# Cross-attention on one core: the first shift in halves, outputs two batches behind, products with V in one block a batch

## The reference

```python
Q = (query @ Wq.T + bq).reshape(B, Sq, N_HEADS, D_K).transpose(0, 2, 1, 3)
K = (key_value @ Wk.T + bk).reshape(B, Skv, N_HEADS, D_K).transpose(0, 2, 1, 3)
V = (key_value @ Wv.T + bv).reshape(B, Skv, N_HEADS, D_K).transpose(0, 2, 1, 3)
scores = jnp.einsum('bhqd,bhkd->bhqk', Q.astype(jnp.float32), K.astype(jnp.float32))
scores = scores / np.sqrt(D_K)
attn = jax.nn.softmax(scores, axis=-1)
context = jnp.einsum('bhqk,bhkd->bhqd', attn, V.astype(jnp.float32)).astype(query.dtype)
...
output = context @ W_o.T + b_o
x = output + query
mu = jnp.mean(x, axis=-1, keepdims=True)
var = jnp.mean(jnp.square(x - mu), axis=-1, keepdims=True)
return (x - mu) / jnp.sqrt(var + LN_EPS) * ln_gamma + ln_beta
```

## Time and profile before

| | us |
|---|---|
| median of 3 runs | 155.61 (154.75 to 156.13) |
| profiled execution, whole | 157.02 |
| its span on the core | 155.2 |

### The profile page before, as it was taken

One profiled execution on the slowest core, in us unless ns is written; L12 is line 12 of the kernel. 1 busy time (PEld: TensorE's weight loads), 2 busy tenths in 40 slices (PEclk: granted clock), 3 DMA queues, 4 the chain that ended last, 5 costly groups with the idle time before them and its releaser, 6 DMA issues.

```text
span 155.2 us, 3853 instructions
## 1 busy us (share of the span) xinstructions
PE 134.0 (86%) x1466; PEld 116.7 (75%) x1466; DVE 105.6 (68%) x247; ACT 80.4 (52%) x163; POOL 60.7 (39%) x83
## 2 busy tenths in 40 slices
PE   5799989679979999889998998999899996779850
PEld 4599779468768899769988987899787875667620
DVE  6745997757937769947896699578779887031252
ACT  3648437214426666526655666465656565566410
POOL 8946997920003998404140504130023023041051
PEclk9999999987999999999999999999999999999997
DMA  4976989698950250697414050405031001001002
GB/s 128 358 259 216 269 296 227 159 270 239 301 204 2 102 156 0 169 267 235 135 52 151 4 178 4 155 2 183 24 128 34 4 4 30 4 4 30 4 0 59
DMA packets 14354, 19.58 MB, mean 126 GB/s; under 512 B 2192, under 2 KB 13520, under 8 KB 14336
## 3 DMA queue, kind: packets, MB, share of 16 engines
q1 hardware_dynamic: 13056, 17.26, 35.6%
q0 software_dynamic: 592, 1.70, 4.5%
q10 hardware_dynamic: 688, 0.38, 0.8%
HBM read 6.30 MB, written 0.92 MB: 47 GB/s over the span
## 4 chain that ended last, share of the span: by engine, by line
PE 65%; DVE 11%; DMA 10%; ACT 6%; issue 5%; SPq 1%; POOLq 0%; ACTq 0%; DVEq 0%
PE m_bank L793 19%; PE pv_bank L873 12%; PE st_bank L857 11%; PE mx_bank L834 10%; DMA q_stack<-shift 6%; DVE mx L656 6%; PE m_bank L901 4%; DMA c_raw<-ctxT 3%; PE m_bank L884 2%; ACT pw L561 2%; PE st_bank L793 2%; DMA q_stack<-q_first 1%; DVE q_hl L618 1%; PE m_bank L841 1%; ACT o_normT L552 1%
## 5 line engine op out<-in xcount | busy, mean ns | idle before, releaser
L656 DVE TENSOR_REDUCE mx<-mx_bank 112x1 f32<-112x375 f32 x128 | 64.6, 541 | 20.4 <-PE mx_bank L834 19.8
L561 ACT ACTIVATE pw<-st_bank 125x448 f32<-125x448 f32 x90 | 48.5, 548 | 48.5 <-PE st_bank L857 47.7
L834 PE MATMUL mx_bank<-k_stack,q_stack 128*112 128x376 f32 x128 | 41.3, 351 | 2.2 <-DVE mx L656 1.2
L857 PE MATMUL st_bank<-q_stack,k_stack 128*125 128x224 f32 x180 | 37.7, 294 | 1.7 <-DMA q_stack<-shift 1.7
L857 PEld LDWEIGHTS st_bank<-q_stack,k_stack 128*125 128x125 f32 x180 | 30.0, 190 | 5.5 <-issue 3.0
L834 PEld LDWEIGHTS mx_bank<-k_stack,q_stack 128*112 128x112 f32 x128 | 22.0, 181 | 4.5 <-DVE mx L656 2.4
L359 POOL TENSOR_TENSOR c_hl<-c_raw,c_hl 128x752 fp32r<-128x752 f32 x6 | 10.9, 1814 | 27.5 <-DVE c_hl L612 27.5
L873 PE MATMUL pv_bank<-pw,v_sb 125*17 125x112 f32 x720 | 20.4, 260 | 1.1 <-ACT o_raw L535 1.1
L405 POOL TENSOR_SCALAR var_eps<-mv 112x1 f32<-112x1 f32 x7 | 1.6, 223 | 49.2 <-DVE mv L692 49.2
L793 PE MATMUL m_bank<-c_hl,w_hl 128*128 128x376 f32 x84 | 18.7, 365 | 0.9 <-ACT w_hl L449 0.9
L873 PEld LDWEIGHTS pv_bank<-pw,v_sb 125*17 125x17 f32 x720 | 16.3, 97 | 3.9 <-issue 2.2
(11 more groups left out here) (102 smaller groups left out, 160.6 us busy)
## 6 DMA issues: line engine op xcount, KB each, us to landing
k_stack<-k_hl SPq DMA_DIRECT2D x48, 188.0 KB, 2.5
c_raw<-ctxT SPq DMA_DIRECT2D x8, 375.0 KB, 4.3
q_stack<-q_hl SPq DMA_DIRECT2D x6, 224.0 KB, 4.5
q_stack<-q_hl SPq DMA_DIRECT2D x6, 168.0 KB, 3.4
x_space<-x_nat POOLq DMA_DIRECT2D x1, 896.0 KB, 10.3
out<-yo SPq DMA_DIRECT2D x8, 112.0 KB, 1.9
pw<-wT SPq DMA_DIRECT2D x2, 256.0 KB, 4.8
x_space<-xT SPq DMA_DIRECT2D x1, 448.0 KB, 6.1
```

The lines of the kernel that those rows point to most:

```text
L561: nc.scalar.activation(p_tile[0:KC, n % PR, :, :], st_of(n)[0:KC, 0:4 * Q].rearrange("p (j q) -> p j q", j=4), ACT.Exp, scale=float(DK) ** ...
L656: nc.vector.tensor_reduce(mx[b % 2][:, h % 2, q_pair(h // 2):q_pair(h // 2) + 1], mx_bank[n % MR][0:Q, 0:KV], axis=AX_X, op=ALU.max, negat ...
L834: nc.tensor.matmul(mx_bank[n % MR][0:Q, 0:KVP], q_stack[k][:, side, q_pair(h // 2), b - Q_STACKS[k][0], :], k_stack[b % 3][:, h // 2, :], ...
L857: last = nc.tensor.matmul(st_of(n)[0:KC, k * 2 * Q:(k + 1) * 2 * Q], k_stack[i % 3][:, 2 * g + k, c * KC:(c + 1) * KC], q_stack[qk][:, :, ...
```

## The change

**Order tables.** P's ring gets fourteen tiles. yo is dropped (z is scaled in place), which frees the space.

```diff
-PR = 3 * NC
+PR = UNITS + 2
...
-U_K = (0, 2)
-U_V = (3, 5, 8)
-U_OT, U_ONT, U_OUT = 5, 9, 11
-U_BIAS = 4
-U_Q = (5, 10)
-U_NEGATE, U_MT, U_SHIFT = 5, 7, 9
-U_CONTEXT = 7
-HEADS = (1, 1, 2, 1, 2, 1, 1, 1, 2, 1, 2, 1)
...
+U_OUT, U_OT, U_BIAS = 2, 8, 1
+U_K = (3, 5)
+U_V = ((11, 11, 11), (10, 11, 11), (9, 10, 11))
...
+NORM_WITH = {3: 0, 4: 1, 5: 2, 6: 4, 7: 5}
+U_MT = (11, 9, 6, 6, 6, 6, 6)
+U_NEGATE = (10, 8, 5, 5, 5, 5, 5)
...
+EARLY_HEADS = 14
...
+FIRST_JOBS = {1: (("MT", 0, 1), ("V", 2, 0)), 2: (("V", 2, 1),), 3: (("V", 2, 2),), 4: (("Q", 2, 0),), 5: (("Q", 2, 1),)}
+FIRST_K = (6, 8)
...
-FIRST_HEADS = (2, 3, 2, 3, 2)
+HEADS = (2, 1, 1, 1, 2, 1, 1, 1, 2, 1, 2, 1)
+FIRST_HEADS = ((2, 1, 2, 2, 2, 2, 2, 2, 2, 1, 1, 1), (2, 2, 2, 2, 2, 2, 2, 1, 2, 2, 2, 2))
```

```diff
+            def negate_half(t):
+
+                dve.wait_ge(max_read, H // 2 * (t + 1))
+                src = mx[0][:, :, t:NP:2]
+                hi = neg_half[t][:, :, 0, :]
+                nc.vector.tensor_tensor(hi, src, src, op=ALU.max).then_inc(neg_hi, 1)
+                dve.wait_ge(neg_hi, t + 1)
+                nc.vector.tensor_tensor(neg_half[t][:, :, 1, :], src, hi.bitcast(F32), op=ALU.subtract).then_inc(neg_ready, 1)
...
+            def take_shift_half(t):
+                src = wait_full(dve, "MT", 0, t)
+                nc.vector.tensor_copy(shift_half[t][:, :], src[0:2 * NP, 0:Q]).then_inc(shift_ready, 1)
...
+            def stack_shift_half(t):
+
+                act.wait_ge(shift_ready, t + 1)
+                for side in range(2):
+                    act.dma_start(q_stack[0][SPREAD - 1:2 * SPREAD:SPREAD, side, t:NP:2, 0, :].bitcast(F32),
+                                  shift_half[t][NP * side:NP * (side + 1), :].bitcast(F32)).then_inc(half_in[t], 16)
...
-            stack_shift(0)
-            v_part(2, 1)
+            stack_shift_half(0)
+            v_part(1, 1)
+            context_hi(3)
+            for t in range(2):
+                k_hi_part(2, t)
...
-            negate(0)
-            take_shift(0)
...
+                if n == H // 2 - 1:
+                    negate_half(0)
+                if n == H // 2 + 1:
+                    take_shift_half(0)
+                if n == 12:
+                    k_lo_part(2, 0)
...
+            def transpose_max_half(t):
+                dst, full = claim("MT", 0, t)
+                pe.wait_ge(neg_ready, t + 1)
+                nc.tensor.transpose(dst[0:2 * NP, 0:Q], neg_half[t][:, :, :, :].rearrange("q s l a -> q (s l a)").bitcast(F32),
+                                    ident[0:Q, 0:Q]).then_inc(full, 1)
...
-                if u == 0:
-                    pe.wait_ge(shift_in[i % 2], 16 * (i // 2 + 1))
+                if i == 0 and u % HALF == 0:
+                    pe.wait_ge(half_in[u // HALF], 32)
+                if i >= 1 and u == 0:
+                    pe.wait_ge(shift_in[i % 2], 16 * ((i + 1) // 2))
```

```diff
+            def subtract_k(b, t):
+
+                pool.wait_ge(k_hi, 2 * b + t + 1)
+                nc.gpsimd.tensor_tensor(k_hl[b % 2][:, 1, t, :], k_full[:, t, :], k_hl[b % 2][:, 0, t, :].bitcast(F32),
+                                        op=ALU.subtract).then_inc(k_lo, 1)
...
+            def take_k(b, t):
+
+                src = wait_full(act, "K", b, t)
+                if b > AHEAD:
+                    act.wait_ge(k_lo, 2 * (b - 1) + t + 1)
+                nc.scalar.activation(k_full[:, t, :], src[:, 0:KVP], ACT.Identity,
+                                     bias=bqk[:, 2 + t:3 + t]).then_inc(k_taken, 1)
+                act.wait_ge(k_taken, 2 * (b - AHEAD) + t + 1)
+                act.wait_ge(k_in[(b - 2) % 3][t], 48 * ((b - 2) // 3 + 1))
+                nc.scalar.copy(k_hl[b % 2][:, 0, t, :], k_full[:, t, :]).then_inc(k_hi, 1)
```

```diff
+                if b in NORM_WITH:
+                    norm_columns(dst, NORM_WITH[b])
...
-                    elif u % (2 * NC) == 1 + late and n > 2 and not (i == B - 1 and u > 2):
-                        for group in (n // NC - 2, n // NC - 1):
-                            values(*divmod(group, NG))
...
+                    elif u == (1 if i < B - 1 else 2) and i >= 1:
+                        for group in range(NG):
+                            values(i - 1, group)
+                    if i == 0:
+                        for kind, *at in FIRST_JOBS.get(u, ()):
+                            projects[kind](*at)
+                    if u == U_BIAS and i == 1:
+                        bias_of_values()
+                    if u == U_OUT and 3 <= i <= 5:
+                        out_project(i - 3)
+                    if u == U_OT and 1 <= i <= 4:
                         transpose_o(i - 1)
...
+                    if u == 4 and i in (5, 6):
+                        transpose_o(i - 1)
+                    if u == 4 and i == 5:
+                        transpose_o_norm(3)
+                    if i + 1 < B and u == U_MT[i]:
                         transpose_max(i + 1)
...
+                    if u == 7 and i == 5:
+                        out_project(3)
+                    if u == 10 and i >= 5:
+                        out_project(i - 1)
+                    if u == 5 and i == B - 1:
+                        transpose_o(B - 2)
+                    if u == 8 and i == B - 1:
+                        transpose_o_norm(B - 2)
```

```diff
+                    if u == 1 and i == 0:
+                        stack_shift_half(1)
...
+                    if u == (2 if i < B - 1 else 3) and i >= 1:
+                        take_o(i - 1)
+                    if u == (6 if i == 0 else 2) and i + AHEAD + 1 < B:
+                        context_hi(i + AHEAD + 1)
+                    if u in (FIRST_K if i == 0 else U_K) and i + AHEAD < B:
+                        take_k(i + AHEAD, (FIRST_K if i == 0 else U_K).index(u))
+                    if i + 1 < B and u == min(U_MT[i] + 1, UNITS - 1):
                         stack_shift(i + 1)
...
+                        if i + 1 in NORM_WITH:
+                            take_o_norm_t(NORM_WITH[i + 1], "MT", i + 1)
+                    if u == 5 and i == 5:
+                        take_o_norm_t(3, "ONT", 3)
+                    if u == 8 and i == B - 1:
+                        take_o_norm_t(B - 2, "ONT", B - 2)
...
+                pool.wait_ge(rstd_ready, b + 1)
+                nc.gpsimd.tensor_scalar(z[b % 2][:, :], z[b % 2][:, :], mv[b % 2][:, 0:1], rstd[:, 0:1],
+                                        op0=ALU.subtract, op1=ALU.mult).then_inc(y_ready, 1)
...
+                    if u == U_OUT and 3 <= i <= 5:
+                        layer_norm(i - 3)
+                    if i + 1 < B and u == U_NEGATE[i]:
+                        negate(i + 1)
+                    if i + 1 < B and u == U_MT[i]:
+                        take_shift(i + 1)
+                    if u == U_OT and 1 <= i <= 4:
...
-                        negate(i + 1)
+                    if u == 4 and i in (5, 6):
+                        normalise(i - 1)
+                    if u == 5 and i == B - 1:
+                        normalise(B - 2)
+                    if u == 7 and i == 5:
+                        layer_norm(3)
+                    if u == 10 and i in (5, 6):
+                        layer_norm(i - 1)
```

271 lines of the change are left out of this document (124 added, 147 removed).

## The result

The change makes the kernel slower. Four executions took 165.2 to 167.5 us, median 166.15; four of the kernel before, taken on the same chip beside them, have the median 155.69. The ratio is 1.069, with a 95% interval from 1.059 to 1.078. Forecast were 156.0 and a range that ended at 158.6. The profiled execution took 165.2, with a span of 163.3 us against 155.2. Some executions of every kernel run at a lower granted clock and take longer: the ratios and intervals leave them out, the medians do not.

What follows compares the result with a forecast made beforehand. TensorE's work and few waits bound batches 2 to 4, VectorE nearly batch 5, chains batches 6 and 7. Batch 6 at 124.2 + 23.2 + tail 8.2 = 155.6 against 155.2; median 155.61 + 0.4 = 156.0, range 152.8 to 158.6.

Steps and rivals of the forecast that it cites:

- The price list and the walk through the queue: Whole kernel: unit costs read from the trace, walked through TensorE's queue batch by batch; span 155.6 us.
- the start: Before the loop: the first half-shift, issued at 24.7, lets batch 0 begin at 28.9 us instead of 32.92.
- The o_normT waits: In front of output projections: waits for ScalarE's copy, 0.7 us each, 3.5 in five places, disappear in batches 2 to 4.
- The second step of K: ScalarE, units 2 to 5: an added cast of each K half out of SBUF, taken as 0.5 us.
- exp is late at unit 8: Batches 2 to 4: TensorE's shifted-score pair waits for ScalarE's exp, 0.7 to 0.8 us, 1.0 in batch 2.
- The layer norms do pile up: Batch 5: three layer norms instead of one, 1.0 us each on VectorE, make it 14.4 us against 11.23.
- GpSimd's new work ... is hidden.: Ten subtractions (0.9 us each) and seven row scalings on GpSimd cost nothing, since their results are read much later.
- I leave the lower clock in: + 1.7.: Batch 0: the half-rate stretch of the kernel before stays, adding 1.7 us, to 19.8 in all.
- waits of 1.8 and 1.75 in batch 0: TensorE waits 1.8 us for the first half-shift before batch 0, 1.75 at the second half's transposition.
- Landing 3.6.: Start: the first half-shift takes 3.6 us from issue to use, plus 0.6 for the second issue.
- The slower rival: ScalarE becomes the bound, with 8.2 us more work bunched behind the product block; median 159.0, chance 0.28.
- Faster, same and slower: Outcomes against the kernel before: faster case 153.5 (0.30), own sum 156.0 (0.42), slower 159.0 (0.28), regrouped by 1% bounds.

Runs made afterwards that it cites:

- bare run: The profiled execution of e_quiet_fill: the changed kernel with nearly all GpSimd hold-ups, transfers in the way of shifts and clock falls taken away; median 156.16 us.
- e_bias_late: Changed kernel with GpSimd's eight bias additions put behind the subtractions of K in batch 1; median 164.98 us, ratio 1.057.
- e_probe_ts: Kernel before plus idle GpSimd operations on one tile and two numbers beside VectorE's split of the maxima; one execution, 154.68 us.
- e_split: Changed kernel with the products with V of batches 1 to 6 in two blocks, at units 1 and 3; median 173.74 us, ratio 1.114.
- e_quiet: Changed kernel with late bias additions, GpSimd's subtraction waiting for the first half's split, and x loaded in batch 2; median 161.05 us, ratio 1.031.
- e_quiet_fill: e_quiet plus idle matmuls on TensorE in front of four waits (10, 4, 6, 3); median 156.16 us, ratio 1.002.
- e_fill: Changed kernel plus idle matmuls in front of five long TensorE waits (15, 4, 7, 8, 4); median 163.89 us, ratio 1.041.
- e_one_transfer: Changed kernel with each half-shift sent as one transfer instead of two; median 165.09 us, ratio 1.052.
- e_k_back: Changed kernel with K's low part for batches 3 to 7 back on VectorE, ScalarE in one step, no GpSimd subtraction; median 167.48 us, ratio 1.069.

## Why the prediction was wrong, step by step

**What held.** The price list and the walk through the queue. In the bare run batch 0 took 17.98 (the sum without lost clock was 18.1), batch 1 17.32 (17.3), batches 2 to 4 43.26 (43.8), batch 5 14.41 (14.4), batches 6 and 7 23.71 (23.2), the tail 8.20 (8.2). Only the start did not come out, 30.52 against 28.9. That the bare span of 155.4 agrees with the forecast 155.6 is luck in part: the forecast holds 1.7 of lost clock that the bare run does not have, and 1.6 less for the start. The o_normT waits went. The second step of K costs 0.51 (taken as 0.5) and exp is late at unit 8 by 0.47 (taken as 0.7 to 0.8). That ScalarE would become the bound did not happen. The layer norms do pile up in batch 5.

```profile
L397 POOL TENSOR_TENSOR k_hl<-k_full,k_hl 128x376 fp32r<-128x376 f32 x10 | 10.1, 1028 | 0.6 <-ACT k_hl L501 0.6
L501 ACT CAST k_hl<-k_full 128x376 fp32r<-128x376 f32 x10 | 5.1, 507 | 0.3
```

**"GpSimd's new work ... is hidden."** This step failed first, and it is the largest part in the profile: batch 1, 3.2 us over the forecast. It asked whether anybody waits for GpSimd's results; nobody does. It did not ask what GpSimd's operands keep VectorE from. In the kernel before every split of the loop stands clear of GpSimd's two-tile work, and each part takes 0.17 in batches 1 to 7. The change put additions and subtractions over it in batches 1, 2 and 5: 1.61, 0.84 and 0.45 us more. Only the first and last reach TensorE, in the waits of 1.63 and 1.89. Of the 1.89 it is 0.45; the rest is VectorE's work in batch 5, which the forecast had. e_bias_late, without the meeting in batch 1, gave back 2.7 us of that batch: 1.1 of waiting and the fall of the clock behind it. The Trainium skill states this coupling (SBUF — State Buffer, Who interferes with whom: a VectorE instruction with two SBUF inputs contends with a GpSimd instruction that reads SBUF, and whoever is first holds the shared pair for the whole instruction). The trace agrees for two-tile operations and not for one-tile ones, which read SBUF too and did not delay the split (e_probe_ts). It goes beyond "the whole instruction" where GpSimd's operations follow without a gap: 4.10 us over four of them (e_split). The rule spoke against this change, and it was the one to weigh.

**"I leave the lower clock in: + 1.7."** Mis-sized. The forecast had one fall in the loop; there were three, 6.7 us of full-rate work lost. It forecast the waits of 1.8 and 1.75 in batch 0 and did not ask whether the new waits further on could each bring a fall. Here falls followed waits of 3.31, 1.63 and 1.89 us; the wait of 1.09 at 138.95 had none. Nor does a wait of that length always bring one: e_quiet has the same 1.89 in batch 5 at clock 1.00. That pair also gives a price: batch 5 lasted 15.30 with the fall and 14.42 without, 0.9 us. In batch 0 it was 2.1 (20.12 against 17.98). For all falls together the runs give bounds only: about 2.1 of the 4.2 us between the profiled executions of e_quiet and e_quiet_fill, at most 4.1 of the 4.9 between their medians.

**"Landing 3.6."** Mis-sized: 4.2 with the second issue, and 5.92 measured from the first issue to landing. The term carried over the price of one transfer at another moment; with one transfer the first half took 4.36. The second half's landing had no term at all. It is issued at 34.2 behind 1.1 MB of K, 0.9 MB of x and 0.6 MB of weights and constants, all issued since 28.6, and 0.75 MB of context follow it. In five profiled executions TensorE waited for it, 2.3 to 4.2 us (e_fill, e_bias_late, e_one_transfer, e_k_back, e_split), and began unit 6 at 42.5 to 44.6, 8.5 to 10.2 us behind the issue. In that of the kernel after the half landed just as unit 6 began, at 41.55 (7.3 us), and the lost clock hid the time until then. That it also made the slowest execution of the kernel after, 167.5, is likely but not shown.

**Chances.** The slower rival (0.28) had the sign but the wrong mechanism: its sign to look for, a wait above 1.3 us for exp, never came (0.8 at most). Faster, same and slower had 0.33, 0.37 and 0.30, with an upper bound at 158.6. All bounds had been drawn from durations of the kernel before, in which no two engines disturb one another at these places. Three couplings of the same sign, unpriced or priced too low, lay outside them. The range also left out its own slower case: 158.6 is below that rival's 159.0.

## What to carry to other kernels

Where work moves to GpSimd, lay its two-tile operations over VectorE's two-input operations on SBUF in the timeline, not only over their consumers: a small operation on the path can stand still for as long as GpSimd has such work back to back (4.10 us here instead of 0.17). Where a wait is put into dense TensorE work, price it twice, once as the wait and once as a possible fall of the clock (0.9 and 2.1 us in the two places where it could be read here); idle matmuls into a free bank are a cheap test. A small transfer on the path is priced by what is issued in the microseconds ahead of it, on all queues, not by its size (14 KB landed in 2.0 us and in 9.05).

## What the runs showed of the hardware

VectorE was kept out by GpSimd for 4.10 us over four operations (e_split) and for 3.75 over five (e_one_transfer), though each of them is a separate instruction; between operations that wait for one another (0.08 us apart) it got in at once, 0.51 to 0.53 us instead of 0.17. A GpSimd operation on one tile and two numbers did not keep it out at all. VectorE's maxima from PSUM kept 0.55 beside any of it.

A 7 KB transfer alone in ScalarE's queue landed 10.15 us after its issue (e_one_transfer), with 2.6 MB issued on other queues in the four microseconds ahead of it; 14 KB took 2.0 us with no other transfer under way. Another queue was no protection.

TensorE shows gaps of 0.6 to 1.3 us labelled "issue" in or behind blocks of 96 products, in some executions and not in others of the same kernel (0.57 at 146.26 in the kernel after, none in e_quiet_fill). What they are wasn't tested. Elsewhere the label can hide a plain wait: 3.83 us in front of a transposition in e_split, and 0.86 in e_k_back, end 0.1 us behind the split of the maxima.
